# Loading two 128-row weight slabs per transfer, and softmax in one piece with a two-task lag, in a transformer block on eight cores

## The chip, the cores and the metric

The kernel runs on all 8 NeuronCores of one Trainium2 chip. Each core handles one batch element's half of the rows: cores 2b and 2b+1 share batch element b, and each owns 1024 of its 2048 tokens (interleaved blocks of 128). There is no communication between cores; each core computes K and V for all 2048 tokens itself. The metric is device time in microseconds of the slowest core.

A core has a matrix engine (PE; its weight loads are shown as PEld), a vector engine (DVE), a scalar engine (ACT), a general engine (POOL, GpSimd) and a sync engine (SP). In this kernel SP and POOL issue all the DMAs. SBUF is the on-chip memory, PSUM the eight banks into which PE accumulates.

## The reference

For x of shape (4, 2048, 4096), 16 heads of 256:

```python
q, k, v = x @ Wq, x @ Wk, x @ Wv              # rotary on the first 64 of the 256 of each head of q, k
logits  = einsum('bhqd,bhkd->bhqk', q, k)     # causal mask, then / sqrt(256)
out     = einsum('bhqk,bhkd->bhqd', softmax(logits), v)
x = layernorm(x + out @ Wo)
w = kernel * 2.0 - 1.0                        # kernel is a matrix of booleans
x = layernorm(x + scale * (x @ w))
```

The weights are 4096 x 4096, float32 (the last one one byte per entry). Softmax is over up to 2048 keys, with the maximum subtracted.

## The kernel before

Two arenas of SBUF are cut up by hand: `A` holds bfloat16 activations, `B` (`Bu`, `Bf`, `Bb` are views of it as bytes, float32 and bfloat16) holds staging buffers. The order of the work is written out in one walk through the program; each engine gets its instructions in the order of that walk and waits on semaphores for named milestones, so every engine, and each of the two DMA-issuing queues (SP and POOL), runs strictly in that order.

**Projections (lines 239 to 402).** The transposed input, 32 slabs of 128 rows by 2048 tokens, is loaded by POOL in 128 transfers of 128 x 512 float32 into two alternating buffers, and ACT casts each piece to bfloat16 in `A` (L247), where it stays. Then, for each of 8 pairs of heads, five blocks follow: Q, K of either head, V for tokens 0 to 1023, V for tokens 1024 to 2047. A block is 32 steps (`kk`). A step loads a weight slab of 128 rows (SP; 128 x 512 float32 for Q and V, 128 x 256 for K) into one of two staging buffers, DVE casts it into one of two bfloat16 buffers (L269, L320, L371), and PE runs 8 matmuls of 512 columns on it, one for each PSUM bank (L278, L330, L380). The load of step kk waits for the cast of kk-2; the cast waits for its load and for the matmuls of kk-2. After step 31 DVE copies the eight banks to SBUF (L291, L343, L393), and POOL writes the result to DRAM (`qspill`, `kspill`, `vspill`). The first cast of the next block stands behind those eight copies on DVE. During the first Q block the matmuls also wait for the cast of the input slab.

**Attention (lines 407 to 622).** A task is one head and one block of 128 queries, `jj` = 0 to 7; it has (jj+1) x 128 keys in either of two halves P = 0, 1. Logits of both halves go to four PSUM banks (`PL`), the masks being added by a matmul with an identity (L479, L490). DVE takes the negated maximum of each half (L504, L507) and the minimum of the two (L522); ACT computes exp of each half with its row sum (L530); DVE adds the sums (L536), takes the reciprocal (L540) and scales (L546, with bf16 in and out). Three tasks later PE transposes the result in groups of four (L569), DVE copies each group (L579), PE multiplies with V (L592) into two banks, and ACT copies these out (L601). The logits of half P wait for exp of half P of the task before. Q, K and V of a head are loaded two heads ahead by POOL, which also does the rotary arithmetic, six operations of 64 x 1024 and 64 x 2048 per head (L438 to L455), beginning at task jj = 3.

**Output projection, norm, FFN, norm (lines 624 to 908).** Wo (L645, L653) and the FFN weight (L805, L813) are worked through like the projection weights, 8 blocks of 32 steps, with 256 KB (Wo) or 64 KB (FFN) per load, and the cast on ACT. The eight banks of a block are combined with the residual by DVE (L675, L841), whose loads stand in SP's queue ahead of the next block's weights. Between and after them, two passes normalise the rows.

Of the kernel before, what the change touches and what calls it, by code (L numbers as in the profile page):

```python
# [96 lines left out]
def build_nc(taps=()):  # L97
# [100 lines left out]
    def walk():  # L198
# [52 lines left out]

        for p in range(8):
            h0 = 2 * p
            for kk in range(KD):
                b = kk % 2
                if kk >= 2:
                    w = [("qcast", p, kk - 2)]
                elif p > 0:
# [6 lines left out]
                wc = [("qwd", p, kk)]
                if kk >= 2:
                    wc.append(("qmm", p, kk - 2))
                op("vector",
                   lambda e, b=b: e.tensor_copy(Bb[:, WQBF + b * 512:WQBF + (b + 1) * 512],  # L269
                                                Bf[:, WQST + b * 512:WQST + (b + 1) * 512]),  # L270
                   waits=wc, ms=("qcast", p, kk))
# [760 lines left out]
```

How the kernel before makes its waits and increments, by code:

```python
    def op(self, engname, fn, waits=(), inc=None, ms=None):  # L62
        if self.mode == "count":
            for k in waits:
                assert k in self.ms, f"wait on undefined milestone {k}"
            if inc is not None:
                s, n = inc
                self.cnt[s] = self.cnt.get(s, 0) + n
                if ms is not None:
                    for k in (ms if isinstance(ms, list) else [ms]):
                        assert k not in self.ms, f"dup milestone {k}"
                        self.ms[k] = (s, self.cnt[s])
            else:
                assert ms is None, ms
            return
        if engname != self.engname:
            return
        for k in waits:
            s, v = self.ms[k]
            if v > self.waited.get(s, 0):
                self.eng.wait_ge(self.sems[s], v)
                self.waited[s] = v
        instr = fn(self.eng)
        if inc is not None:
            s, n = inc
            instr.then_inc(self.sems[s], n)
# [1 line left out]
    def final_wait(self, engname, semname):  # L88
        if self.mode == "count" or engname != self.engname:
            return
        v = self.cnt.get(semname, 0)
        if v > self.waited.get(semname, 0):
            self.eng.wait_ge(self.sems[semname], v)
            self.waited[semname] = v
```

## Time and profile before

| | us |
|---|---|
| three timed runs | 5691.8, 5708.56, 5713.06 |
| the profiled execution, its own time | 5640.55 |
| its span on the slowest core (core 6) | 5639.0 |
| spans of the other cores | 5549.1 to 5633.0 |
| PE, DVE, ACT, POOL busy on core 6 | 4048.0, 1579.5, 686.4, 611.0 |

All durations below are from the profiled execution, on core 6. A time of the form 3509.66 is a position in it, in us from its start. A busy PE is not a PE at its peak, since its matmuls overlap and their ends are modelled: the granted clock of a stretch (1.00 is 2.4 GHz, 0.50 is 1.2 GHz) and the number of matmuls that fit into it say more. Idle time of an engine counts only where the others wait for it.

### The profile page before, as it was taken

The numbers are of one execution on the slowest core, as the hardware profiler recorded it, in microseconds if no ns is written. First come the engines' busy times: TensorE is split into PE (matmuls) and PEld (weight loads), VectorE is DVE, ScalarE is ACT, GpSimd is POOL, SyncE is SP. The second block draws the span as 40 slices with busy tenths as digits, with TensorE's granted clock in tenths as the row PEclk, the third lists the DMA queues.
The fourth block names the chain that finished last, engine by engine and source line by source line (L and its number), as shares of the span: only waits on it lengthen the run. The fifth ranks groups of instructions, "written<-read, shape, count | busy, mean of one in ns | idle before, by whom it ended". The sixth has DMA issues, their size and how long they took to land.

```text
span 5639.0 us, 60269 instructions; the slowest of 8 cores (5549.1 to 5639.0 us)
## 1 busy us (share of the span) xinstructions
PE 4048.0 (72%) x19074; PEld 1861.7 (33%) x19074; DVE 1579.5 (28%) x3310; ACT 686.4 (12%) x1505; POOL 611.0 (11%) x644
## 2 busy tenths in 40 slices
PE   3369898998988889898994555555587773488850
PEld 0123343333333333333332343333433331233320
DVE  0012222222222222222223555555401114322222
ACT  2210000000000000000001222222222222222210
POOL 2200000000000000000004333333000001100011
PEclk6579999889889999988886676667799996699975
DMA  4433434244342433424233111111055555422246
GB/s 130 128 99 116 133 105 137 84 120 122 99 134 85 136 114 115 135 91 132 88 114 108 44 44 53 56 44 44 1 157 166 167 170 178 131 91 90 90 128 188
DMA packets 349225, 615.17 MB, mean 109 GB/s; under 512 B 41970, under 2 KB 140274, under 8 KB 346866
## 3 DMA queue, kind: packets, MB, share of 16 engines
q1 hardware_dynamic: 295666, 420.45, 26.0%
q0 software_dynamic: 53248, 190.88, 9.7%
q8 instruction: 159, 2.61, 0.2%
q14 instruction: 152, 1.25, 0.1%
HBM read 495.81 MB, written 109.05 MB: 107 GB/s over the span
## 4 chain that ended last, share of the span: by engine, by line
PE 48%; DMA 26%; DVE 11%; issue 8%; ACT 6%; DVEq 0%; POOL 0%; SPq 0%; ACTq 0%; POOLq 0%
PE PL L330 9%; PE pb L330 9%; DMA arenaB<-wo 7%; DMA arenaB<-wv 6%; PE PL L380 5%; PE pb L380 5%; DMA arenaB<-wq 5%; DMA arenaB<-xT 4%; PE PL L813 4%; PE PL L479 4%; PE pb L813 4%; PE pb L592 3%; DMA out<-arenaB 2%; ACT arenaB L530 2%; PE pb L569 1%
## 5 line engine op out<-in xcount | busy, mean ns | idle before, releaser
L380 PE MATMUL PL<-arenaB,arenaA 128*128 128x512 bf16 x2048 | 575.0, 407 | 109.6 <-DVE arenaB L371 108.1
L330 PE MATMUL PL<-arenaA,arenaB 128*128 128x512 bf16 x2048 | 573.5, 406 | 86.7 <-DVE arenaB L320 86.7
L330 PE MATMUL pb<-arenaA,arenaB 128*128 128x512 bf16 x2048 | 568.6, 403 | 0.0
L380 PE MATMUL pb<-arenaB,arenaA 128*128 128x512 bf16 x2048 | 566.2, 402 | 0.0
L530 ACT ACTIVATE arenaB<-PL,arenaB 128x128 bf16<-128x128 f32 (+7 forms) x256 | 188.8, 750 | 2727.7 <-DVE arenaB L522 2727.7
L278 PE MATMUL PL<-arenaA,arenaB 128*128 128x512 bf16 x1024 | 305.7, 427 | 293.1 <-ACT arenaA L247 219.8
L371 DVE CAST arenaB<-arenaB 128x512 bf16<-128x512 f32 x512 | 217.0, 426 | 757.9 <-DMA arenaB<-wv 479.8
L320 DVE CAST arenaB<-arenaB 128x256 bf16<-128x256 f32 x512 | 148.9, 293 | 778.7 <-PE pb L330 722.0
L653 PE MATMUL PL<-arenaB,arenaA 128*128 128x512 bf16 x1024 | 273.2, 390 | 119.4 <-ACT arenaB L645 79.8
L813 PE MATMUL PL<-arenaB,arenaA 128*128 128x512 bf16 x1024 | 272.9, 390 | 93.6 <-DVE arenaB L831 38.4
L380 PEld LDWEIGHTS PL<-arenaB,arenaA 128*128 128x128 bf16 x2048 | 200.7, 102 | 408.7 <-issue 273.7
L330 PEld LDWEIGHTS PL<-arenaA,arenaB 128*128 128x128 bf16 x2048 | 209.2, 103 | 365.3 <-issue 203.9
L479 PE MATMUL PL<-arenaA 128*128 128x512 bf16 (+3 forms) x528 | 175.2, 475 | 192.7 <-ACT arenaB L530 144.3
L278 PE MATMUL pb<-arenaA,arenaB 128*128 128x512 bf16 x1024 | 303.2, 424 | 0.0
L330 PEld LDWEIGHTS pb<-arenaA,arenaB 128*128 128x128 bf16 x2048 | 210.3, 103 | 275.2 <-issue 110.2
L380 PEld LDWEIGHTS pb<-arenaB,arenaA 128*128 128x128 bf16 x2048 | 210.3, 103 | 275.4 <-issue 102.2
L269 DVE CAST arenaB<-arenaB 128x512 bf16<-128x512 f32 x256 | 108.5, 427 | 652.2 <-PE pb L278 376.6
L813 PE MATMUL pb<-arenaB,arenaA 128*128 128x512 bf16 x1024 | 270.2, 386 | 0.7 <-DVE arenaB L841 0.6
L653 PE MATMUL pb<-arenaB,arenaA 128*128 128x512 bf16 x1024 | 269.6, 387 | 0.0
L278 PEld LDWEIGHTS PL<-arenaA,arenaB 128*128 128x128 bf16 x1024 | 99.4, 104 | 466.5 <-issue 390.8
L592 PE MATMUL pb<-arenaA 128*128 128x128 bf16 x1584 | 145.8, 267 | 123.4 <-DVE arenaA L579 91.7
L645 ACT CAST arenaB<-arenaB 128x512 bf16<-128x512 f32 x256 | 158.0, 617 | 435.2 <-DMA arenaB<-wo 395.4
(95 smaller groups left out, 3491.6 us busy)
## 6 DMA issues: line engine op xcount, KB each, us to landing
arenaB<-wv SPq DMA_DIRECT2D x512, 256.0 KB, 2.9
arenaB<-wq SPq DMA_DIRECT2D x256, 256.0 KB, 2.9
arenaB<-wk SPq DMA_DIRECT2D x512, 128.0 KB, 2.1
arenaB<-wo SPq DMA_DIRECT2D x256, 256.0 KB, 2.9
arenaB<-xT POOLq DMA_DIRECT2D x128, 256.0 KB, 3.8
z_hbm<-arenaB POOLq DMA_DIRECT2D x128, 256.0 KB, 3.5
arenaB<-z_hbm SPq DMA_DIRECT2D x128, 256.0 KB, 3.4
kspill<-arenaB POOLq DMA_DIRECT2D x16, 1024.0 KB, 6.8
```

The lines of the kernel that those rows point to most:

```text
L269: lambda e, b=b: e.tensor_copy(Bb[:, WQBF + b * 512:WQBF + (b + 1) * 512], Bf[:, WQST + b * 512:WQST + (b + 1) * 512]),
L278: lambda e, b=b, m=m, n=n, kk=kk: e.matmul(bank(m * 2 + n), Bb[:, WQBF + b * 512 + m * 128:WQBF + b * 512 + (m + 1) * 128], A[:, kk * 2048 ...
L320: lambda e, b=b: e.tensor_copy(Bb[:, WKBF + b * 256:WKBF + (b + 1) * 256], Bf[:, WKST + b * 256:WKST + (b + 1) * 256]),
L330: lambda e, b=b, m=m, n=n, kk=kk: e.matmul(bank(m * 4 + n), Bb[:, WKBF + b * 256 + m * 128:WKBF + b * 256 + (m + 1) * 128], A[:, kk * 2048 ...
L371: lambda e, b=b: e.tensor_copy(Bb[:, WVBF + b * 512:WVBF + (b + 1) * 512], Bf[:, WVST + b * 512:WVST + (b + 1) * 512]),
L380: lambda e, b=b, c=c, bidx=bidx, kk=kk: e.matmul(bank(bidx), A[:, kk * 2048 + c * 128:kk * 2048 + (c + 1) * 128], Bb[:, WVBF + b * 512:WVB ...
L479: qb=qb, kb=kb, jj=jj, stop=stop, AR=AR: e.matmul(PL[:, pbase + coff:pbase + coff + csz], AR[:, qb + m * 1024 + jj * 128:qb + m * 1024 + ( ...
L530: op("scalar", lambda e, P=P, KW=KW, SVX=SVX, AUB=AUB: e.activation(Bb[:, AUB + P * KW:AUB + (P + 1) * KW], PL[:, P * 1024:P * 1024 + KW], ...
L592: lambda e, dh=dh, c=c, kk=kk, KK=KK, vb=vb, AT=AT, AR=AR: e.matmul(avP[dh][:, 0:128], AR[:, vb + c * 256 + dh * 128:vb + c * 256 + (dh + ...
L645: lambda e, b=b: e.copy(Bb[:, WOBF + b * 512:WOBF + (b + 1) * 512], Bf[:, WOST + b * 512:WOST + (b + 1) * 512]),
L653: lambda e, m=m, b=b, kk=kk: e.matmul(bank(m), A[:, CAT0 + kk * 1024 + m * 128:CAT0 + kk * 1024 + (m + 1) * 128], Bb[:, WOBF + b * 512:WOB ...
L813: lambda e, m=m, b=b, kk=kk: e.matmul(bank(m), A[:, X2T0 + kk * 1024 + m * 128:X2T0 + kk * 1024 + (m + 1) * 128], Bb[:, FWBF + b * 512:FWB ...
```

## The change

1. Projections, Wo and FFN: a step loads and casts two slabs (256 rows) at once, with twice the bytes per transfer and twice the columns per cast, and 16 matmuls follow; the number of steps per block falls from 32 to 16. There are still two staging buffers and two cast buffers, each twice as large. The input comes in 64 transfers of 128 x 1024.
2. The staging area for K results is one buffer instead of two, and V results are written to DRAM after each half of a pair (four writes of half the size instead of two).
3. Attention: one maximum over both halves, one exp over both halves with one sum; the minimum of two maxima and the sum of two sums are gone. The logits of both halves wait for the whole exp of the task before.
4. Attention: transposes and V matmuls follow two tasks after the logits instead of three, and ACT's copy-out of a task stands behind the exp of the newer task instead of ahead of it.

On ACT, at the start of attention, before (L530 is exp, L601 the copy-out; both halves and both banks are counted together):

```order
L530 ACTIVATE arenaB<-PL,arenaB 128x128 x2
L530 ACTIVATE arenaB<-PL,arenaB 128x256 x2
L530 ACTIVATE arenaB<-PL,arenaB 128x384 x2
L601 CAST arenaA<-pb 128x128 x2
L530 ACTIVATE arenaB<-PL,arenaB 128x512 x2
L601 CAST arenaA<-pb 128x128 x2
L530 ACTIVATE arenaB<-PL,arenaB 128x640 x2
```

and after (L544 is exp, L613 the copy-out):

```order
L544 ACTIVATE arenaB<-PL,arenaB 128x256
L544 ACTIVATE arenaB<-PL,arenaB 128x512
L544 ACTIVATE arenaB<-PL,arenaB 128x768
L613 CAST arenaA<-pb 128x128 x2
L544 ACTIVATE arenaB<-PL,arenaB 128x1024
L613 CAST arenaA<-pb 128x128 x2
L544 ACTIVATE arenaB<-PL,arenaB 128x1280
```

The rows look alike, but the first copy-out before is that of task 0, emitted in the same turn as the exp of task 3, which follows it; after, it is also that of task 0, but emitted in the turn of task 2, whose exp stands ahead of it. So an exp no longer stands behind the V matmuls that PE runs in the same turn.

On DVE, within one head, before:

```order
L540 RECIPROCAL arenaB<-arenaB 128x1
L546 TENSOR_SCALAR arenaA<-arenaB 128x256
L504 TENSOR_REDUCE arenaB<-PL 128x1
L507 TENSOR_REDUCE arenaB<-PL 128x1
L579 COPY arenaA<-pb 128x512 x3
L579 COPY arenaA<-pb 128x256
L522 TENSOR_TENSOR arenaB<-arenaB 128x1
L536 TENSOR_TENSOR arenaB<-arenaB 128x1
L540 RECIPROCAL arenaB<-arenaB 128x1
L546 TENSOR_SCALAR arenaA<-arenaB 128x512
```

and after:

```order
L550 RECIPROCAL arenaB<-arenaB 128x1
L556 TENSOR_SCALAR arenaA<-arenaB 128x256
L527 TENSOR_REDUCE arenaB<-PL 128x1
L589 COPY arenaA<-pb 128x512 x4
L550 RECIPROCAL arenaB<-arenaB 128x1
L556 TENSOR_SCALAR arenaA<-arenaB 128x512
```

Two reductions have become one over both halves, the two TENSOR_TENSORs are gone, and the group copies are those of the task two back, not three.

The diff, cut to its core (the K and V blocks change as the Q block does, the FFN weights as Wo):

```diff
-        for ii in range(128):
-            kk, qq = ii // 4, ii % 4
+        for ii in range(64):
+            kk, hf = ii // 2, ii % 2
             b = ii % 2
-            w = [("xcast", ii - 2)] if ii >= 2 else [("tabq",)]
-            dma("gpsimd", Bf[:, XST + b * 512:XST + (b + 1) * 512],
-                xT_d[kk * 128:(kk + 1) * 128, qq * 512:(qq + 1) * 512],
+            w = [("xcast", ii - 2)] if ii >= 2 else []
+            dma("gpsimd", Bf[:, XST + b * 1024:XST + (b + 1) * 1024],
+                xT_d[kk * 128:(kk + 1) * 128, hf * 1024:(hf + 1) * 1024],
                 waits=w, ms=("xdma", ii))
...
-            for kk in range(KD):
-                b = kk % 2
-                if kk >= 2:
-                    w = [("qcast", p, kk - 2)]
+            for k2 in range(16):
+                b = k2 % 2
+                if k2 >= 2:
+                    w = [("qcast", p, k2 - 2)]
...
+                dma("sync", Bf[:, WQST + b * 1024:WQST + (b + 1) * 1024].rearrange("p (c m) -> p c m", m=512),
+                    wq_d[k2 * 256:(k2 + 1) * 256, h0 * HD:h0 * HD + 512].rearrange("(c p) m -> p c m", p=128),
+                    waits=w, ms=("qwd", p, k2))
+                wc = [("qwd", p, k2)]
+                if k2 >= 2:
+                    wc.append(("qmm", p, k2 - 2))
                 op("vector",
+                   lambda e, b=b: e.tensor_copy(Bb[:, WQBF + b * 1024:WQBF + (b + 1) * 1024],
+                                                Bf[:, WQST + b * 1024:WQST + (b + 1) * 1024]),
+                   waits=wc, ms=("qcast", p, k2))
+                for sub in range(2):
+                    kk = 2 * k2 + sub
...
+                for hh in range(2):
+                    h = h0 + hh
+                    dma("gpsimd",
+                        vspill[h].rearrange("p (c d) -> p c d", d=HD)[:, ps * 8:(ps + 1) * 8, :],
...
-            wlog.append(("expp", t - 1, P) if t > 0 else p1done)
+            wlog.append(("exp", t - 1) if t > 0 else p1done)
...
             op("vector", lambda e, KW=KW, SVX=SVX: e.reduce_max(
-                   Bf[:, SVX:SVX + 1], PL[:, 0:KW], axis=AX.X, negate=True),
-               waits=wmx, ms=("mxa", t))
-            op("vector", lambda e, KW=KW, SVX=SVX: e.reduce_max(
-                   Bf[:, SVX + 1:SVX + 2], PL[:, 1024:1024 + KW], axis=AX.X, negate=True),
-               waits=[("lgp", t, 1), ("mxa", t)], ms=("mxb", t))
+                   Bf[:, SVX:SVX + 1],
+                   PL.rearrange("p (c k) -> p c k", k=1024)[:, :, 0:KW],
+                   axis=AX.XY, negate=True),
+               waits=wmx, ms=("mx", t))
...
+            op("scalar", lambda e, KW=KW, SVX=SVX, AUB=AUB: e.activation(
+                   Bb[:, AUB:AUB + 2 * KW].rearrange("p (c k) -> p c k", k=KW),
+                   PL.rearrange("p (c k) -> p c k", k=1024)[:, :, 0:KW],
+                   AF.Exp, bias=Bf[:, SVX:SVX + 1], scale=1.0,
+                   accum_out=Bf[:, SVX + 5:SVX + 6]),
+               waits=wexp, ms=("exp", t))
...
-        for u in range(T2 + 3):
+        for u in range(T2 + 2):
...
-            if u - 3 >= 0:
-                emit_trav(u - 3)
+            if u - 2 >= 0:
+                emit_trav(u - 2)
             if u < T2:
                 emit_smx(u)
+            if u - 2 >= 0:
+                emit_avev(u - 2)
...
-            for kk in range(KD):
-                b = kk % 2
-                if kk >= 2:
-                    w = [("wocast", nn, kk - 2)]
+            for k2 in range(16):
+                b = k2 % 2
+                if k2 >= 2:
+                    w = [("wocast", nn, k2 - 2)]
```

## Rows read from the trace of the kernel before

**Rows 1.** The cores of the profiled execution: span, and mean granted TensorE clock.

```profile
core 4: 5558.1 us, clock 0.838
...
core 6: 5639.0 us, clock 0.811
```

**Rows 2.** Stretches of core 6: busy us (x instructions) PE, PEld, DVE, ACT, POOL; granted clock, DMA share, GB/s.

```profile
0.00:349.00 349.00, 114.72 (x259) 33.44 (x260) 19.48 (x47) 79.99 (x129) 69.09 (x132) 0.57 0.44 124
349.00:2993.00 2644.00, 2379.85 (x9984) 1006.80 (x9982) 642.35 (x1550) 0.00 (x0) 38.72 (x46) 0.91 0.38 114
...
3042.00:4073.00 1031.00, 565.90 (x4333) 391.19 (x4332) 558.81 (x1072) 239.64 (x756) 339.00 (x194) 0.66 0.13 45
```

**Rows 3.** Single blocks of 256 matmuls (K, Q, K, Wo), columns as in rows 2.

```profile
1007.00:1065.00 58.00, 57.48 (x255) 25.52 (x256) 9.41 (x33) 0.00 (x0) 1.43 (x2) 0.95 0.28 87
...
934.00:1002.00 68.00, 59.83 (x256) 25.09 (x256) 13.15 (x32) 0.00 (x0) 2.26 (x2) 0.95 0.51 151
1070.00:1138.00 68.00, 67.21 (x256) 27.82 (x256) 9.66 (x33) 0.00 (x0) 0.71 (x1) 0.81 0.26 82
4167.00:4231.00 64.00, 59.30 (x256) 23.73 (x256) 2.19 (x4) 19.14 (x31) 1.22 (x3) 0.98 0.52 154
```

**Rows 4.** First block, timeline: start us, us, engine, line, op, out<-in, [idle before <-releaser].

```profile
106.73 1.21 ACT L247 CAST arenaA<-arenaB 128x512 bf16<-128x512 f32 x2 [3.58 <-DMA arenaB<-xT]
...
107.96 1.13 POOL L210 DMA_DIRECT2D arenaB<-xT  x2 [3.66 <-ACT arenaA L247]
112.31 0.62 ACT L247 CAST arenaA<-arenaB 128x512 bf16<-128x512 f32 x1 [4.37 <-DMA arenaB<-xT]
```

**Rows 5.** Projection blocks after the first, DMA issues: queue, count, KB each, median us to landing.

```profile
arenaB<-wv SPq DMA_DIRECT2D x512, 256.0 KB, 2.9
arenaB<-wk SPq DMA_DIRECT2D x510, 128.0 KB, 2.1
...
qspill<-arenaB POOLq DMA_DIRECT2D x16, 512.0 KB, 4.4
```

**Rows 6.** Between two projection blocks, timeline.

```profile
796.63 2.48 DVE L343 CAST arenaB<-PL 128x512 bf16<-128x512 f32 x4 [3.23 <-PE pb L330]
...
801.42 0.75 DVE L371 CAST arenaB<-arenaB 128x512 bf16<-128x512 f32 x2
...
801.98 0.58 PE L380 MATMUL PL<-arenaB,arenaA 128*128 128x512 bf16 x1 [5.53 <-DVE arenaB L371]
```

**Rows 7.** Matmul groups: line, engine, op, out<-in, xcount | busy, mean ns | idle before <-releaser.

```profile
L380 PE MATMUL PL<-arenaB,arenaA 128*128 128x512 bf16 x2048 | 575.0, 407 | 109.6 <-DVE arenaB L371 108.1
L330 PE MATMUL PL<-arenaA,arenaB 128*128 128x512 bf16 x2048 | 573.5, 406 | 86.7 <-DVE arenaB L320 86.7
...
L278 PE MATMUL PL<-arenaA,arenaB 128*128 128x512 bf16 x1024 | 305.7, 427 | 293.1 <-ACT arenaA L247 219.8 <-DVE arenaB L269 72.9
```

**Rows 8.** One attention task of 256 keys per half, timeline.

```profile
3508.16 0.42 DVE L507 TENSOR_REDUCE arenaB<-PL 128x1 f32<-128x256 f32 x1
...
3509.66 2.41 PE L592 MATMUL pb<-arenaA 128*128 128x128 bf16 x28
...
3512.48 0.49 ACT L530 ACTIVATE arenaB<-PL,arenaB 128x256 bf16<-128x256 f32 x1
...
3513.20 0.48 PE L479 MATMUL PL<-arenaA 128*128 128x384 bf16 x2 [1.14 <-ACT arenaB L530]
```

**Rows 9.** Attention, twelve heads, DVE groups by shape.

```profile
L522 DVE TENSOR_TENSOR arenaB<-arenaB 128x1 f32<-128x1 f32 x96 | 52.4, 546 | 0.0
...
L536 DVE TENSOR_TENSOR arenaB<-arenaB 128x1 f32<-128x1 f32 x97 | 46.5, 480 | 307.9 <-ACT arenaB L530 307.9
...
L504 DVE TENSOR_REDUCE arenaB<-PL 128x1 f32<-128x1024 f32 x12 | 14.7, 1222 | 0.0
```

**Rows 10.** Attention, twelve heads, ACT groups by shape.

```profile
L530 ACT ACTIVATE arenaB<-PL,arenaB 128x1024 bf16<-128x1024 f32 x25 | 27.7, 1117 | 0.0
```

**Rows 11.** Between two Wo blocks, timeline.

```profile
4167.16 1.44 PE L653 MATMUL PL<-arenaB,arenaA 128*128 128x512 bf16 x3 [11.83 <-ACT arenaB L645]
```

More of the change, by code:

```diff
@@ new lines, in walk @@
+                wc = [("wod", nn, k2)]
+                if k2 >= 2:
+                    wc.append(("womm", nn, k2 - 2))
+                op("scalar",
+                   lambda e, b=b: e.copy(Bb[:, WOBF4 + b * 1024:WOBF4 + (b + 1) * 1024],
+                                         Bf[:, WOST4 + b * 1024:WOST4 + (b + 1) * 1024]),
+                   waits=wc, ms=("wocast", nn, k2))
+                for sub in range(2):
+                    kk = 2 * k2 + sub
+                    for m in range(8):
+                        wmm = [("wocast", nn, k2), p2done]
+                        if kk == 0 and nn > 0:
+                            wmm.append(("zev", nn - 1, m))
+                        op("tensor",
+                           lambda e, m=m, b=b, sub=sub, kk=kk: e.matmul(
+                               bank(m),
+                               A[:, CAT0 + kk * 1024 + m * 128:CAT0 + kk * 1024 + (m + 1) * 128],
+                               Bb[:, WOBF4 + b * 1024 + sub * 512:WOBF4 + b * 1024 + (sub + 1) * 512],
+                               start=(kk == 0), stop=(kk == KD - 1)),
+                           waits=wmm if (kk == 0 or m == 0) else (),
+                           ms=("womm", nn, k2) if (m == 7 and sub == 1) else None)
@@ new lines, in walk @@
+                wc = [("fwd", nn, k2)]
+                if k2 >= 2:
+                    wc.append(("fmm", nn, k2 - 2))
+                op("scalar",
+                   lambda e, b=b: e.copy(Bb[:, FWBF6 + b * 1024:FWBF6 + (b + 1) * 1024],
+                                         Bu[:, FWST6 + b * 1024:FWST6 + (b + 1) * 1024]),
+                   waits=wc, ms=("fwcast", nn, k2))
+                for sub in range(2):
+                    kk = 2 * k2 + sub
+                    for m in range(8):
+                        wmm = [("fwcast", nn, k2), x2tall]
+                        if kk == 0 and nn > 0:
+                            wmm.append(("z2ev", nn - 1, m))
+                        op("tensor",
+                           lambda e, m=m, b=b, sub=sub, kk=kk: e.matmul(
+                               bank(m),
+                               A[:, X2T0 + kk * 1024 + m * 128:X2T0 + kk * 1024 + (m + 1) * 128],
+                               Bb[:, FWBF6 + b * 1024 + sub * 512:FWBF6 + b * 1024 + (sub + 1) * 512],
+                               start=(kk == 0), stop=(kk == KD - 1)),
+                           waits=wmm if (kk == 0 or m == 0) else (),
+                           ms=("fmm", nn, k2) if (m == 7 and sub == 1) else None)
```

365 lines of the change are left out of this document (161 added, 204 removed).

## The prediction

> **What bounds the kernel now.** I read the cores first [rows 1]: their spans follow the granted clock, and core 6, at 0.811, sets the end, 81 us behind core 4. Then the stretches of core 6 [rows 2]. The reader is to see three regimes. Up to 349 us PE is busy a third of the time while 128 input pieces come in: that is the first Q block. From 349 to 2993 us PE is busy 90%, at clock 0.91: 39 more blocks of 256 matmuls. From 3042 to 4073 us, 128 attention tasks at 8.05 us each, every engine is idle nearly half the time or more, PE at 0.66 clock: a chain of waits, no full engine.
>
> Single blocks [rows 3] say what is left in the dense stage. A K block takes 57.5 us at 0.95, which is PE's own pace (256 x 0.213 at full clock, plus a slow start). The same block at 0.81 takes 67.2. The Q block shown is 68 us long with only 59.8 of PE busy: 8 us of waiting for weights. The Wo block is 64 us with 4.7 idle. K loads are half as large and land in 2.1 us, Q and V loads in 2.9 [rows 5]. With two buffers, load plus cast (2.9 + 0.43 and a wait or two) come to 3.5 us or so, and the two steps of PE that have to hide them last 3.4. So Q, V and Wo stand exactly at the edge, K does not.
>
> **The change, part by part.**
>
> *Input and first Q block.* The chain of a buffer is cast, issue, transfer, cast. In [rows 4] two casts run from 106.73, the first ends at 107.35, POOL starts the next transfers at 107.96 (0.6 later), and the next cast starts at 112.31. Over the block a pair of pieces costs (349 - 6 for the gap that ends it - 17 for the start, my estimate) / 64 = 5.1 us. After, 32 pairs of 512 KB are left. The nearest row for such a transfer is the Q spill, two of 512 KB one behind the other on the same queue: 4.4 us each [rows 5]. The cast of 1024 columns I take as 0.62 + 512 x 0.82 ns = 1.04 us; the slope is that of exp between 256 columns (0.49) [rows 8] and 1024 (1.117) [rows 10]. A pair is then 0.6 + 4.4 + 1.04 = 6.0; I take 6.5, since weights now share the engines in larger pieces. 32 x 6.5 = 208 against 326: **-115 us**. Bounds: -130 (6.0, nothing shared), -40 (if the rate stays near the 124 GB/s of rows 2).
>
> The Trainium skill's page "DMA: Bandwidth & Descriptors", section "Anatomy of one DMA", gives a transfer from POOL 2.0 us plus its bytes at 436 GB/s. By that 512 KB would land in 3.2 us and this term would be -155; but it gives 2.6 us for 256 KB, where rows 4 show 4.35 from issue to cast, so the rows decide.
>
> *Weight stalls.* A line through 128 KB in 2.1 and 256 KB in 2.9 [rows 5] puts 512 KB at 4.5 us, as the spill row has it. Load, cast (two slabs: at most the 0.75 of the pair in rows 6) and waits make about 5.5 us, and two steps of 16 matmuls last 6.8. The stall goes; what is late next is PE itself. How much it is worth: PE idles 86.7 us ahead of K matmuls, all of it gaps between 16 blocks, 5.4 each [rows 7]. V has as many blocks and 109.6, thus 23 of stalls; Q has 72.9 besides the input's 219.8, less 7 gaps of 5.4, thus 35. Idle below the resolution of the pipelined records and the slower clock after a stall come on top: the Q block of rows 3 is 10 us longer than the K block and shows 8 of it as idle, and V blocks stretch without showing it. I take 75. Bounds 40 (58 less what the spills still cost) and 90. **-75 us.**
>
> *Gaps between blocks.* The eight copies of 0.62 stay, the first cast behind them doubles [rows 6]: at most +0.3 for Q and V, +0.15 for K, over 39 gaps **+8 us** (0 to 12). The halved V write and the single K staging buffer add waits on transfers that were issued a block (about 60 us) earlier; the evictions and casts behind them on DVE, and PE behind those, would stand if they were late, but the spill of rows 5 lands in 4.4 us: 0.
>
> *Attention.* Rows 8 show the chain of one task: V matmuls to 3512.07, copy-out, exp from 3512.48, next logits at 3513.20. PE waits 1.13 us here for work that belongs to the other half of the pipeline. After, exp of a task waits only for its maximum and runs beside transposes and V matmuls; PE goes from the last V matmul straight into the next logits. Removed per head of 8 tasks: the step from V matmul to exp, 8 x 0.41 = 3.3; exp of one half until the logits start, 8 x 0.23 plus the eight exps (0.28 + 0.82 ns a column, 4608 columns: 6.0), 7.9. Then the TENSOR_TENSORs on single columns: they take 0.15 and average 0.546 and 0.480 [rows 9], presumably because GpSimd's rotary operations hold them up; 8 x (0.40 + 0.33) = 5.8, of which I count 5. Sum -16.2. Added: the maximum of both halves now starts after both logits. One at 1024 keys takes 1.222 [rows 9], one at 256 takes 0.42 [rows 8], so 0.15 + 1.045 ns a column: +4.8 per head at most; but the second maximum often stood behind the first, or behind the held-up scaling, so I count +2.2. And in tasks 3 to 6 the double exp (0.28 + 1.64 ns per key) lasts longer than the short V product beside it: +1.5. Sum **-12.5 us per head, x 16 = -200**. Bounds: -100 (all 4.8 exposed, held-up scalings as costly as both TENSOR_TENSORs were, exp over the V product by 3), and -290 (PE also gets the full clock: the logits of a head are 18,432 columns, 7.7 us at 2.4 GHz and 15.4 at 1.2). What is late next is PE through logits, transposes and V product, with the maximum and the group copies on DVE in the middle.
>
> *Wo.* A block gets from 64 to 58.6, 8 x 5.4 = -43. Its gap gets longer: PE waits 11.83 us for the first cast [rows 11], whose load is issued behind the residual's loads; 1.6 more to land and 0.4 to cast, 8 x 2.0 = +16. **-27** (-45 to -10).
>
> *FFN.* Loads of 64 KB were hidden, so nothing to gain; +0.9 in each gap for the larger first cast and load: **+7** (0 to 15). The norm passes are unchanged.
>
> Sum: -115 - 75 + 8 - 200 - 27 + 7 = -402 us. The profiled execution took 5640.5, so it would take 5238. It lies 68 us under the median of the timed runs, 5708.6; I subtract from the median and predict **5305 us**.
>
> **The rivals.**
>
> *The clock takes it back (slower).* At 0.81 a block costs 67.2 instead of 57.5 [rows 3], 9.7 us. There are 56 dense blocks (40 projection, 8 Wo, 8 FFN); core 6 ends 81 us behind core 4 [rows 1], which is what 8 such blocks cost. If denser matmuls bring 0.81 to the other 48, that is +466: 5305 + 466 = 5771, slower. It decides from 41 more blocks (402 / 9.7). For it: the second K block of rows 3 shows that the dense stages are subject to it. Against: full-clock blocks already run at PE's pace, so the change makes them little denser, and the 5.5 us gaps stay.
>
> The Trainium skill's page "TensorE: Matmul & The Clock Gate", section "Part 1: The HAM clock gate", says that a whole die goes to 13/16 of the clock once three of its cores run dense matmuls, and stays there while the load lasts. By that rule all four cores of a die would already stand at 0.81 throughout; rows 3 with two K blocks of one core at 0.95 and 0.81 do not bear that out, and so I leave this rival a small chance.
>
> *Attention gives half or less.* For it: at 640 keys and more per half the double exp and the whole maximum come to over 4 us in series behind the logits. Against: the short chain of rows 8 disappears in every task. It gives 5405.
>
> *Transfers do not scale.* If two 512 KB transfers land no faster per byte than four of 256 KB, the input gives 40 and stalls 30 of their 75: +120, 5425. Against: K's 2.1 and the spill's 4.4.
>
> *Attention at full clock.* Shorter gaps on PE keep it at 2.4 GHz: -60 to -90 more, 5230.
>
> **How the numbers follow.** The forecast as it stands 0.56; attention half or transfers not scaling 0.22 together; full clock 0.16; the clock rival 0.04; something unseen that ends near zero 0.02. Bounds of the terms, taken at their ends together, give 5140 and 5540; nobody expects them all at once, so the range is 5200 to 5440. Three timed runs span 21 us, so 0.5% (28 us) is about what can be told from no change. Faster by more than that 0.94, within 0.02, slower 0.04.
>
> **What would show it.** First Q block: PE's idle time on ACT's input casts from 219.8 to about 110, and the block ending near 235 us. Loads of 512 KB landing in 4 to 5 us. Q and V blocks as long as K's at equal clock, near 57.5. Attention near 830 us, exp no longer behind the copy-out, PE going from V matmul to logits in under 0.3 us in long tasks. Gaps ahead of Wo near 14 us. The prediction is wrong if transfers of 512 KB need 6 us or more, if logits still wait for exp over 1 us in most tasks, or if over half the blocks take 67 us.

## The result, and the profile after

The changed kernel took 5256.56 us in the median of 9 runs (4962.88 to 5603.46), the kernel before 5710.81 (10 runs, 5592.54 to 5924.43). Both medians contain executions in which some cores had a lower clock; the ratio leaves these out: **0.8825, 95% interval 0.8693 to 0.8957**. On the median of before, 5708.56, that is 5038 us: 671 less, where the forecast was 402 less, and outside its range. The direction was right, the size was not.

The cores, as in [rows 1]:

```profile
core 2: 4961.3 us, clock 0.880
...
core 7: 4942.7 us, clock 0.881
```

All eight end within 19 us of each other. In the profile of before, core 6 spent 586 us at a granted clock of 0.8125 and core 4 none, which are the 81 us between them. So the two profiled spans differ by 678 us, but only 597 of it (core 4's 5558.1 to core 2's 4961.3) can come from the edit. I account for these 597.

The stretches of core 2, columns as in [rows 2]: first block, 39 blocks, the way to the first logits, attention, the start of Wo, Wo, norm pass, FFN, end.

```profile
0.00:234.00 234.00, 98.98 (x253) 30.63 (x258) 16.79 (x31) 68.14 (x65) 34.13 (x68) 0.70 0.62 186
234.00:2690.50 2456.50, 2226.66 (x9784) 992.61 (x9984) 542.64 (x928) 0.00 (x0) 51.98 (x62) 0.96 0.40 123
2690.50:2736.00 45.50, 0.90 (x7) 0.43 (x6) 4.88 (x8) 0.00 (x0) 25.11 (x17) 0.56 0.29 89
2736.00:3429.00 693.00, 446.05 (x4428) 333.68 (x4475) 425.31 (x704) 222.07 (x510) 343.57 (x194) 0.85 0.19 66
...
3435.50:4002.00 566.50, 455.35 (x2007) 203.84 (x2048) 75.37 (x112) 132.75 (x127) 30.30 (x56) 0.91 0.56 171
4002.00:4211.00 209.00, 37.59 (x257) 22.33 (x258) 117.29 (x233) 45.00 (x82) 38.87 (x72) 0.51 0.58 177
4211.00:4766.00 555.00, 459.49 (x2007) 204.30 (x2046) 103.73 (x169) 131.47 (x127) 30.22 (x56) 0.91 0.28 85
4766.00:4961.00 195.00, 0.14 (x1) 0.00 (x0) 52.71 (x103) 3.98 (x16) 39.38 (x72) 0.51 0.60 189
```

The same stretch of attention in before, on the undisturbed core 4:

```profile
2947.00:3999.00 1052.00, 559.26 (x4443) 396.35 (x4474) 573.21 (x1088) 243.40 (x766) 338.46 (x194) 0.67 0.13 44
```

The reader is to see the fourth row of after beside this one. PE, DVE and ACT are busy for fewer us, GpSimd for as many as before. PE's 4,400 matmuls shrink from 559 to 446 us, though no matmul went: the granted clock rose from 0.67 to 0.85. The span shrank by 359, more than any engine's busy time did. What went is mostly waiting.

Against the terms of the sum (core 4 of before, core 2 of after; a block is from its first weight load to its last, means):

| term | before | after | measured | forecast |
|---|---|---|---|---|
| first Q block | 315.8 | 208.2 | -108 | -115 |
| 7 Q, 16 V, 16 K blocks | 63.76, 60.22, 56.98 | 56.83, 56.83, 56.88 | -104 | -75 |
| 39 gaps (Q, K, V) | 6.03, 6.04, 6.11 | 6.16, 6.22, 6.42 | +9 | +8 |
| attention, first logits to last V matmul | 1052.5 | 693.4 | **-359** | **-200** |
| Wo stage (block, gap) | 62.97, 12.92 | 56.71, 16.07 | -28 | -27 |
| FFN stage (block, gap) | 57.6, 12.99 | 57.2, 13.86 | +3 | +7 |

Together -587; the other 10 lie in the start, the last gap and the end, a few us each. Over all cores the median of attention goes from 1042 to 692 us, -350; the experiments below use these medians, with 16 heads of 8 tasks in each.

The DMA issues, as in [rows 5], with the input pieces:

```profile
arenaB<-wv SPq DMA_DIRECT2D x256, 512.0 KB, 4.1
arenaB<-wq SPq DMA_DIRECT2D x128, 512.0 KB, 4.3
arenaB<-wk SPq DMA_DIRECT2D x256, 256.0 KB, 2.8
arenaB<-wo SPq DMA_DIRECT2D x128, 512.0 KB, 4.1
arenaB<-xT POOLq DMA_DIRECT2D x64, 512.0 KB, 4.9
```

And PE's matmul groups, as in [rows 7]:

```profile
L402 PE MATMUL PL<-arenaB,arenaA 128*128 128x512 bf16 x2007 | 540.0, 390 | 95.8 <-DVE arenaB L391 93.6
L347 PE MATMUL PL<-arenaA,arenaB 128*128 128x512 bf16 x2006 | 539.7, 390 | 91.1 <-DVE arenaB L335 88.9
...
L291 PE MATMUL PL<-arenaA,arenaB 128*128 128x512 bf16 x1005 | 287.2, 410 | 158.3 <-ACT arenaA L258 109.9
```

The idle time on the input casts is 109.9, from 219.8. V now idles about as long as K (95.8 and 91.1), which is gaps alone. The mean matmul fell from 407 to 390 ns in V, but also in K, which had no stalls (406 to 390): that is core 6's time at 0.8125. The same two groups of before on core 4, which had none of it:

```profile
L380 PE MATMUL PL<-arenaB,arenaA 128*128 128x512 bf16 x2007 | 542.7, 392 | 124.8 <-DVE arenaB L371 121.1 <-issue 0.2
L330 PE MATMUL PL<-arenaA,arenaB 128*128 128x512 bf16 x2006 | 540.0, 391 | 88.9 <-DVE arenaB L320 86.7 <-issue 0.2
```

So V's gain is mainly idle time, not clock. Only the Q blocks had a lower clock too: on core 4 the granted clock in them was 0.944 in the mean against 0.962 in the K blocks, and all blocks of core 2 have 0.963 or 0.964 after.

Then the pipeline itself, the timeline of core 2 from a long task (1024 keys a half; the V product at 3035.66, beside its exp, is that of the task two before) into tasks of 128 and 256 keys a half:

```profile
3028.23 4.05 POOL L475 TENSOR_TENSOR arenaB<-arenaB,tabks 64x2048 bf16<-64x2048 bf16 x1
3028.72 4.04 DVE L556 TENSOR_SCALAR arenaA<-arenaB 128x1792 bf16<-128x1792 bf16 x1
...
3032.68 2.28 DVE L527 TENSOR_REDUCE arenaB<-PL 128x1 f32<-128x2048 f32 x1
...
3035.05 1.97 ACT L544 ACTIVATE arenaB<-PL,arenaB 128x2048 bf16<-128x2048 f32 x1 [5.48 <-DVE arenaB L527]
...
3035.66 1.50 PE L602 MATMUL pb<-arenaA 128*128 128x128 bf16 x24
...
3037.25 0.43 ACT L613 CAST arenaA<-pb 128x128 bf16<-128x128 f32 x2
3037.26 0.27 PE L502 MATMUL PL<-arenaA 128*128 128x128 bf16 x2
...
3038.66 0.47 ACT L544 ACTIVATE arenaB<-PL,arenaB 128x256 bf16<-128x256 f32 x1 [0.98 <-DVE arenaB L527]
...
3039.54 1.72 PE L602 MATMUL pb<-arenaA 128*128 128x128 bf16 x28
...
3041.10 0.38 PE L502 MATMUL PL<-arenaA 128*128 128x256 bf16 x2
...
3041.35 0.43 ACT L613 CAST arenaA<-pb 128x128 bf16<-128x128 f32 x2 [2.12 <-PE pb L602]
```

Exp (L544) waits for the maximum and for nothing else, and is over when the V product (L602) ends; the next logits (L502) start as soon as the V product is through, beside the copy-out (L613), where [rows 8] show 1.1 us between them. 28 V matmuls took 2.41 us there and take 1.72 here, at a higher clock. The first two rows show where DVE is still held up longest: a scaling of some 0.7 us that takes 4.04 and ends 0.5 us after GpSimd's rotary operation.

### The profile page after: what moved, and what is told of

Same layout as the page of the kernel before. It is cut to its first block, busy times and chain, and to the rows that moved or that the text cites. A ratio compares the mean times of both kernels' runs of the same rounds, so it can differ in the third digit from the quotient of the medians.

```text
span 4961.3 us, 52305 instructions; the slowest of 8 cores (4942.7 to 4961.3 us)
## 1 busy us (share of the span) xinstructions
PE 3725.5 (75%) x18740; PEld 1788.0 (36%) x19074; DVE 1338.7 (27%) x2286; ACT 604.9 (12%) x929; POOL 593.6 (12%) x596
## 4 chain that ended last, share of the span: by engine, by line
PE 71%; DMA 9%; DVE 9%; issue 6%; ACT 3%; POOL 0%; another core or an unknown queue 0%; DVEq 0%; SPq 0%; ACTq 0%; POOLq 0%
PE PL L402 9%; PE PL L347 9%; PE pb L402 9%; PE pb L347 9%; PE PL L833 5%; PE PL L670 5%; PE pb L833 5%; PE pb L670 5%; PE PL L291 4%; PE pb L291 4%; PE PL L502 4%; DMA arenaB<-xT 3%; PE pb L602 3%; DMA out<-arenaB 2%; DVE arenaB L527 2%
## 5 line engine op out<-in xcount | busy, mean ns | idle before, releaser
L402 PE MATMUL PL<-arenaB,arenaA 128*128 128x512 bf16 x2007 | 540.0, 390 | 95.8 <-DVE arenaB L391 93.6
L347 PE MATMUL PL<-arenaA,arenaB 128*128 128x512 bf16 x2006 | 539.7, 390 | 91.1 <-DVE arenaB L335 88.9
L347 PE MATMUL pb<-arenaA,arenaB 128*128 128x512 bf16 x2007 | 533.2, 386 | 2.7 <-issue 0.7
L402 PE MATMUL pb<-arenaB,arenaA 128*128 128x512 bf16 x2008 | 532.9, 386 | 2.4 <-issue 0.2
L544 ACT ACTIVATE arenaB<-PL,arenaB 128x256 bf16<-128x256 f32 (+7 forms) x128 | 156.3, 1221 | 2879.2 <-DVE arenaB L527 2873.0
L291 PE MATMUL PL<-arenaA,arenaB 128*128 128x512 bf16 x1005 | 287.2, 410 | 158.3 <-ACT arenaA L258 109.9
L670 PE MATMUL PL<-arenaB,arenaA 128*128 128x512 bf16 x1003 | 268.6, 389 | 116.3 <-ACT arenaB L660 100.8
L391 DVE CAST arenaB<-arenaB 128x1024 bf16<-128x1024 f32 x256 | 176.1, 693 | 657.9 <-PE pb L402 597.6
L833 PE MATMUL PL<-arenaB,arenaA 128*128 128x512 bf16 x1003 | 271.6, 392 | 99.7 <-ACT arenaB L823 72.7
L335 DVE CAST arenaB<-arenaB 128x512 bf16<-128x512 f32 x256 | 107.7, 426 | 718.3 <-PE pb L347 686.0
L291 PE MATMUL pb<-arenaA,arenaB 128*128 128x512 bf16 x1003 | 286.6, 410 | 1.3 <-issue 0.4
L833 PE MATMUL pb<-arenaB,arenaA 128*128 128x512 bf16 x1004 | 267.8, 387 | 1.1
L670 PE MATMUL pb<-arenaB,arenaA 128*128 128x512 bf16 x1004 | 266.5, 386 | 1.1
L527 DVE TENSOR_REDUCE arenaB<-PL 128x1 f32<-128x256 f32 (+7 forms) x128 | 173.6, 1356 | 173.0 <-PE pb L579 131.7
L280 DVE CAST arenaB<-arenaB 128x1024 bf16<-128x1024 f32 x128 | 88.2, 694 | 468.4 <-PE pb L291 411.3
L210 POOL DMA_DIRECT2D z_hbm<-arenaB x128 | 69.1, 540 | 1192.2 <-DVE arenaB L851 530.8
L579 PE MATMUL pb<-identb,arenaA 128*128 128x128 bf16 x1152 | 108.9, 233 | 109.3 <-DVE arenaA L589 109.3
```

The source lines that it names most:

```text
L291: lambda e, b=b, sub=sub, m=m, n=n, kk=kk: e.matmul(bank(m * 2 + n), Bb[:, WQBF + b * 1024 + sub * 512 + m * 128: WQBF + b * 1024 + sub * ...
L335: lambda e, b=b: e.tensor_copy(Bb[:, WKBF + b * 512:WKBF + (b + 1) * 512], Bf[:, WKST + b * 512:WKST + (b + 1) * 512]),
L347: lambda e, b=b, sub=sub, m=m, n=n, kk=kk: e.matmul(bank(m * 4 + n), Bb[:, WKBF + b * 512 + sub * 256 + m * 128: WKBF + b * 512 + sub * 25 ...
L391: lambda e, b=b: e.tensor_copy(Bb[:, WVBF + b * 1024:WVBF + (b + 1) * 1024], Bf[:, WVST + b * 1024:WVST + (b + 1) * 1024]),
L402: lambda e, b=b, sub=sub, c=c, bidx=bidx, kk=kk: e.matmul(bank(bidx), A[:, kk * 2048 + c * 128:kk * 2048 + (c + 1) * 128], Bb[:, WVBF + b ...
L527: op("vector", lambda e, KW=KW, SVX=SVX: e.reduce_max(Bf[:, SVX:SVX + 1], PL.rearrange("p (c k) -> p c k", k=1024)[:, :, 0:KW], axis=AX.XY ...
```

## The experiments

Each is told by its attention stage, median over the cores, because the stages are independent (shown by att_all, below). Clock means the granted clock in that stretch, also the median over the cores; a single row shows that of its core. The edits of the attention are three: the **order** (exp ahead of the copy-out on ACT), the **merge** (one maximum and one exp over both halves in place of two, with the TENSOR_TENSORs gone), and the **lag** (two tasks in place of three between logits and V product).

**order_only.** Before, with the copy-out behind exp.

```diff
+        def emit_avev(t):            # the two copy-outs, out of emit_trav
...
                 emit_smx(u)
+            if u - 3 >= 0:
+                emit_avev(u - 3)
```

> The kernel before, with one edit in attention: ACT's copy-out of a task stands behind the exp of the newest task; lag of three tasks, split maximum and split exp stay. The attention stage lasts 1053 us before (core 4) and 693 after the whole change. Theory A (the step from V matmul to exp on ACT was the chain, the rest is small): 780 us or less. Theory B (the parts need each other: exp still waits for the minimum of the maxima, which stands behind the group copies on DVE): only the step V matmul to exp (0.65 us x 8) and the part of exp that fits beside the V matmuls (about 4 us per head) go, 9 us per head, so 905 us.

Measured: 838 us, -204. Core 4:

```profile
2959.40:3792.10 832.70, 486.73 (x4446) 348.60 (x4479) 536.38 (x1088) 243.31 (x766) 341.77 (x195) 0.77 0.16 55
```

It lies between the two theories (780 or less, 905). The order is the largest part, but not all; DVE is as full as before (536 against 573), and the clock is halfway (median 0.76).

**merge_only.** Before, with one maximum and one exp.

```diff
-            op("vector", ... e.reduce_max(..., PL[:, 0:KW], axis=AX.X, negate=True), ...
-            op("vector", ... e.reduce_max(..., PL[:, 1024:1024 + KW], axis=AX.X, negate=True), ...
+            op("vector", ... e.reduce_max(..., PL.rearrange("p (c k) -> p c k", k=1024)[:, :, 0:KW], axis=AX.XY, ...
-            op("vector", ... e.tensor_tensor(..., ALU.min), ...
-            for P in range(2):
+            op("scalar", ... e.activation(..., AF.Exp, bias=Bf[:, SVX:SVX + 1], ...
-            op("vector", ... e.tensor_add(...), ...
```

> The kernel before, with one edit in attention: one maximum and one exp over both halves; copy-out ahead of exp and lag of three stay. Theory A: the two TENSOR_TENSORs that GpSimd holds up are gone, 6 us per head, so about 960 us. Theory B: exp still stands behind the copy-out, and is now twice as long ahead of the next logits (+6 us per head and 0.2 x 8), the maximum is later by up to 4.8, against 6 of held-up TENSOR_TENSORs: 1053 to 1130 us, no gain or slower.

Measured: 960 us, -82, clock 0.73: the figure of theory A. The longer maximum and the longer exp cost less than the removed instructions and their hold-ups gave. In the prediction these parts (-5, +2.2 and +1.5 per head) come to -1.3 per head, or -21 us.

**lag_only.** Before, with a lag of two.

```diff
-            if u - 3 >= 0:
-                emit_trav(u - 3)
+            if u - 2 >= 0:
+                emit_trav(u - 2)
```

> The kernel before, with one edit in attention: transposes and V matmuls follow two tasks after the logits instead of three. Both theories: the same work stands in the same chain, 1053 us within 25. If the lag by itself were the cause, it would be under 1000.

Measured: 1041 us, within 1 us of before, clock 0.65.

**att_all.** Before, with the whole attention change, and nothing else of the edit.

> The kernel before with the whole attention change and its own projections, Wo and FFN. If the stages are independent: attention 693 us within 15, the rest as before, so about 360 us less than before on an undisturbed core. If the larger transfers or the clock of the stages around it had a part in the attention gain: over 720 us.

Measured: 692 us, as in the changed kernel, clock 0.85; what follows attention took 1581 us against 1564 to 1571 in the three runs above. So the input, weight and Wo parts of the edit have no share in the 350, and its size has to be explained within the attention. The whole time fell by less than the 360 expected: the four cores without 0.8125 took 5233 to 5268 us, some 300 less than core 4 of before, mostly because first logits came at 2978 to 2985 us there and not at 2947. The old projections vary like this: over the cores without 0.8125 of all runs that have them, the first block took 288 to 333 us, a Q block 63.5 to 66.3 and a V block 59.8 to 61.5. In the changed kernel these are 202 to 217, and 56.7 to 56.9 for both.

**after_copy_first** and **after_lag3.** The changed kernel, each with one part undone.

```diff
-            if u < T2:
-                emit_smx(u)
             if u - 2 >= 0:
                 emit_avev(u - 2)
+            if u < T2:
+                emit_smx(u)
```

> The changed kernel, with one edit undone: the copy-out of a task stands ahead of the exp of the newest task on ACT. Attention lasts 691 us in the changed kernel; the copy-out order alone took 205 of 1043 from the kernel before, the merging alone 82. Theory interaction (with the merged exp the order is worth more, as the whole 352 is 65 more than the parts): 950 to 970 us, as with merging alone. Theory sum (the parts add): 690 + 205 = 895.

```diff
-            if u - 2 >= 0:
-                emit_trav(u - 2)
+            if u - 3 >= 0:
+                emit_trav(u - 3)
             if u < T2:
                 emit_smx(u)
-            if u - 2 >= 0:
-                emit_avev(u - 2)
+            if u - 3 >= 0:
+                emit_avev(u - 3)
```

> The changed kernel with the lag of three tasks of before. By lag_only (no difference) 691 us of attention within 15. Rival: now that exp runs beside the V product, the pairing counts; with lag two the longest V products stand beside the two shortest exps, with lag three beside the first three and the longest exp beside a short one: +1.5 us per head, 715 us.

Measured: 996 us (+304, more than either expectation) and 720 us (+28, outside the 15 that lag_only had led me to expect, and near the 715 of the rival). The timeline of after_copy_first, core 2:

```profile
3205.28 1.01 PE L602 MATMUL pb<-arenaA 128*128 128x128 bf16 x8 [1.38 <-DVE arenaA L589]
3206.38 0.43 ACT L613 CAST arenaA<-pb 128x128 bf16<-128x128 f32 x2 [5.13 <-PE pb L602]
3206.70 1.13 ACT L544 ACTIVATE arenaB<-PL,arenaB 128x1024 bf16<-128x1024 f32 x1
...
3208.06 1.23 PE L502 MATMUL PL<-arenaA 128*128 128x512 bf16 x4 [1.77 <-ACT arenaB L544]
3208.29 2.02 DVE L556 TENSOR_SCALAR arenaA<-arenaB 128x1024 bf16<-128x1024 bf16 x1
```

V product, copy-out, exp and logits are again one chain, and now the whole exp of both halves (1.13 us, at 1024 keys in all) stands in it, where the split one let PE start after the first half.

With these the effect can be taken apart in one order: before 1042, with the order 838, with the merge as well 720 (after_lag3), with the lag as well 692. That is -204, -118, -28. The merge is worth 82 with the old order and 118 with the new. The lag is worth 1 alone, 28 in the changed kernel, and costs 36 with the merge but the old order (960 to 996). **The parts do not add up one by one**: 204 + 82 + 1 = 287.

**before_no_rotary** and **after_no_rotary.** Is it GpSimd that holds DVE up, and how much of the gain is that?

```diff
-            op("gpsimd", ... e.tensor_mul(Bb[0:64, 7168:9216], AR[0:64, kb:kb + 2048], tabkc[:, :]), ...
+            op("gpsimd", ... e.tensor_mul(Bb[0:64, 7168:7170], AR[0:64, kb:kb + 2], tabkc[:, 0:2]), ...
```

(likewise the other five rotary operations of each head, so all but two columns of Q and K enter the logits unrotated)

> The kernel before with GpSimd's six rotary operations per head cut to two columns each (their DMAs stay), so Q and K are not rotated. Theory GpSimd (DVE's scalings and TENSOR_TENSORs are held up beside them, in tasks 5 and 6 of a head, 10.8 and 12.9 us long where 6.9 and 7.8 would be in line): 9 us per head less, attention about 900 us instead of 1043, and tasks 5 and 6 at 7 to 8 us. Rival (these tasks are long for their size): over 1000.

> The changed kernel with the same six operations cut to two columns. If the change got rid of most of the hold-ups (no TENSOR_TENSORs, the scaling beside logits): 691 down to 660 to 675, so that about 110 of the 352 us gained are hold-ups that went. If the hold-ups are as costly as before: down by 140, to 550.

Measured: 886 us (-156 against 1042) and 668 us (-24 against 692), both as the GpSimd theory had them. The hold-up can be seen in the timeline of before, core 6, DVE and then GpSimd:

```profile
3540.85 1.94 DVE L536 TENSOR_TENSOR arenaB<-arenaB 128x1 f32<-128x1 f32 x1 [2.07 <-ACT arenaB L530]
3542.89 0.16 DVE L540 RECIPROCAL arenaB<-arenaB 128x1 f32<-128x1 f32 x1
3543.16 4.21 DVE L546 TENSOR_SCALAR arenaA<-arenaB 128x1536 bf16<-128x1536 bf16 x1
3547.30 1.08 DVE L504 TENSOR_REDUCE arenaB<-PL 128x1 f32<-128x896 f32 x1
```

```profile
3538.72 4.05 POOL L449 TENSOR_TENSOR arenaB<-arenaA,tabkc 64x2048 bf16<-64x2048 bf16 x1
...
3542.91 4.04 POOL L452 TENSOR_TENSOR arenaB<-arenaB,tabks 64x2048 bf16<-64x2048 bf16 x1
```

An addition of one column takes 1.94 us and ends with the first GpSimd operation shown (both at 3542.8). A scaling starts beside the second and takes 4.21 us, to 0.4 us after that one's end, and the maximum that exp, and so PE's next logits, need is queued behind it. DVE's groups of before (core 4), by shape:

```profile
L522 DVE TENSOR_TENSOR arenaB<-arenaB 128x1 f32<-128x1 f32 x127 | 69.1, 544 | 0.3
...
L546 DVE TENSOR_SCALAR arenaA<-arenaB 128x1536 bf16<-128x1536 bf16 x16 | 56.3, 3516 | 2.1 <-DVE arenaB L540 0.5
L546 DVE TENSOR_SCALAR arenaA<-arenaB 128x1280 bf16<-128x1280 bf16 x16 | 33.7, 2108 | 1.7
```

and of before_no_rotary (core 6):

```profile
L522 DVE TENSOR_TENSOR arenaB<-arenaB 128x1 f32<-128x1 f32 x119 | 17.7, 149 | 0.0
...
L546 DVE TENSOR_SCALAR arenaA<-arenaB 128x1536 bf16<-128x1536 bf16 x15 | 9.3, 620 | 2.0 <-DVE arenaB L540 0.5
L546 DVE TENSOR_SCALAR arenaA<-arenaB 128x1280 bf16<-128x1280 bf16 x15 | 8.3, 553 | 1.6
```

So it is GpSimd; the prediction's "presumably" is shown. And 156 - 24 = 132 us of the 350 are hold-ups that the edit took off the path, with the clock that came back with them (0.67 to 0.75 in before_no_rotary); which of its three parts took them off isn't shown. Some still exist (in after the scaling of 1792 columns takes 3.36 us in the mean, that of 1536 columns 1.41), but they cost only the 24.

**before_filler.** How much of it is the clock? 12 more matmuls of 128 columns per task, which nothing waits for.

```diff
                 emit_trav(u - 3)
+                for i in range(12):
+                    op("tensor", lambda e: e.matmul(pb[0][:, 256:384], identb[:, :], maska[:, :], start=True, stop=True))
```

> The kernel before with twelve matmuls of 128 columns added after the V matmuls of each attention task, into an unused part of a bank; PE runs them while it would wait for the copy-out and exp (a wait of about 1.4 us; they take 0.7 us at full clock, 1.3 at half). In the kernel before attention stands at clock 0.67, in the changed one at 0.85. Theory clock (a third of the gain is that PE, less idle, is granted 2.4 GHz): the clock goes to 0.8 or more and attention gets 40 to 80 us shorter than 1042, with more work. Theory chain only: the clock may rise, but attention stays within 15 us of 1042, since the time is in waits on ACT and DVE.

Measured on core 4:

```profile
2932.50:3945.40 1012.90, 582.72 (x5955) 460.16 (x6004) 559.24 (x1088) 243.12 (x766) 339.55 (x195) 0.80 0.13 46
```

1,536 more matmuls (the trace holds 1,512 of them), and the stage is 28 us shorter (1009 to 1018 on cores 4 to 7, which had no 0.8125; cores 0 to 3 had 1368 to 1794 us of it and are left out). With more to do, PE got 0.80 in place of 0.67. So a busier PE is granted more clock, and that is worth 28 us or more of before's attention; how much more can't be read from this run, since the added matmuls themselves lie partly on the path. The 28 us lie between the two expectations (40 to 80, within 15).

**best1.** The changed kernel with the first load and cast of the next block issued ahead of the evictions of this one, in all dense stages.

```diff
+            if bi + 1 < len(blocks):
+                wload(blocks[bi + 1], 0)
+                wcast(blocks[bi + 1], 0)
+                wload(blocks[bi + 1], 1)
             evict(bk)
...
+            if nn < 7:                 # Wo; FFN likewise
+                wo_lc(nn + 1, 0)
+                wo_lc(nn + 1, 1)
             for m in range(8):
```

> The changed kernel, with the first cast of a projection block ahead of the eight evictions on DVE, and in Wo and FFN the first two loads (and casts) of the next block ahead of the residual's loads. The gaps between blocks are 6.3 us (projections), 16.1 (Wo) and 13.9 (FFN). Theory queue order (the gaps are the cast's and the load's place in their queues): gaps of about 1 us, then PE paced by evictions, 0.6 us a bank in projections and 1.4 to 2 in the others; a period 4 us less in projections, 8 in Wo, 2 in FFN: 39 x 4 + 7 x 8 + 7 x 2 = 226 us less, 4735. Rival (denser matmuls, more of them at 0.81 of the clock, 9.7 us a block): the gain is used up, 4900 to 5000.

Measured: 4840.09 us in the profiled execution against 4962.88, -123. That is half of the 226 expected. First logits come at 2610 in place of 2733 us. Projection gaps went from 6.3 to 1.6 us and blocks grew by 1.4 (by 1.6 in best1_again): 3.1 to 3.3 us a block, 121 to 127 for 39, which is the whole gain. At such a boundary (core 4 of best1_again) PE follows the evictions bank by bank, 0.22 us behind each:

```profile
1007.14 1.03 PE L325 MATMUL pb<-arenaB,arenaA 128*128 128x512 bf16 x4
1009.25 0.38 PE L325 MATMUL PL<-arenaB,arenaA 128*128 128x512 bf16 x1 [1.08 <-DVE arenaB L356]
1009.84 0.38 PE L325 MATMUL PL<-arenaB,arenaA 128*128 128x512 bf16 x1 [0.22 <-DVE arenaB L356]
```

Wo gained little: on core 2 its gap fell from 16.1 to 1.9 us, but each block after the first grew from 56.7 to 69, and the stage went from 566 to 554 us. FFN gained nothing: gap 13.9 to 1.7, block 57.2 to 68.4, stage 555 to 559. The timeline of core 4 of best1 between two Wo blocks:

```profile
3366.16 0.69 DVE L672 TENSOR_TENSOR arenaB<-PL,arenaB 128x512 f32<-128x512 f32 x1 [65.12 <-PE pb L647]
...
3366.96 0.69 DVE L677 BATCH_NORM_STATS2 stats<-arenaB 128x6 f32<-128x512 f32 x1
3367.00 0.38 PE L647 MATMUL PL<-arenaB,arenaA 128*128 128x512 bf16 x1 [1.01 <-DVE arenaB L672]
...
3372.25 0.69 DVE L672 TENSOR_TENSOR arenaB<-pb,arenaB 128x512 f32<-128x512 f32 x1 [0.44 <-DMA z_hbm<-arenaB]
...
3375.48 0.59 PE L647 MATMUL pb<-arenaB,arenaA 128*128 128x512 bf16 x1 [1.81 <-DVE arenaB L672]
```

Each bank comes free only after its residual addition, and DVE has 1.4 us for a bank (0.69 twice), later also a wait for the write of an earlier result. The gap had been waiting for a cast; with that gone, the evictions were next, and they were nearly as late.

**after_again** and **best1_again**, the two kernels beside each other on one chip.

> The changed kernel once more, on the same chip as best1_again, so that the two can be compared with each other. Forecast: its profiled stages repeat within 1%: first logits at about 2735 us, attention 685 to 700 us, a projection block 56.8 us with a gap of 6.2 to 6.4 us behind it.

> The version with the next block's loads and casts issued earlier, beside the changed kernel on one chip. If its gain is the shorter period of the 39 projection blocks (2.9 us each, 113 us in all) and nothing in the other stages, first logits come 120 to 130 us earlier than in the changed kernel here too, and its time is 2.3 to 2.7% shorter. The rival: the first profile of it was taken on another chip, and the 123 us are that chip's; then the two are within 1%.

Measured: ratio to before 0.8874 (0.8831 to 0.8917) for the changed kernel and 0.8672 (0.8627 to 0.8717) for best1; 0.8672 / 0.8874 = 0.977, thus -2.3%. First logits at 2737 and 2616 us. The gain of best1 is real and not another chip's; it beats both kernels.

## Why the prediction was wrong

**The step that failed is the attention term, "Sum -12.5 us per head, x 16 = -200".** Its mechanism was right: exp freed from the copy-out, PE from the V product straight into logits. Its size was not: -22 us per head. It lies beyond the far bound of -290 too. By the parts of a task (core 4 of before, core 2 of after; PE's points are starts of weight loads; means over the heads, summed over the 8 tasks of a head):

| stretch of a task | before | after | difference | forecast |
|---|---|---|---|---|
| first to last weight load of the logits | 13.2 | 10.5 | -2.7 | none |
| from there to the end of the maximum | 21.5 | 16.0 | -5.5 | +2.2, and a part of -5 |
| from there to the last weight load of the V product | 15.9 | 14.3 | -1.6 | +1.5 |
| from there to the next logits | 15.2 | 2.3 | -12.9 | -11.2, and a part of -5 |

1. *The chain behind the V product* was sized about right: 3.3 + 7.9 and part of the 5. order_only and after_copy_first show that it is the chain.
2. *Hold-ups of DVE.* I counted only what [rows 9] show on single columns, 5 us per head. The scalings are held up as well, up to 3.6 us over their length, and the maximum is queued behind them. I had named them ("the held-up scaling") only as cover for the longer maximum. The two no_rotary runs make it 132 / 16 = 8.3 per head, 52 us more than the 80 counted, clock included.
3. *The longer maximum.* Counted +2.2; the stretch became 5.5 shorter. merge_only shows that with the old order too one maximum and one exp win, by 82, where the prediction's terms for them give 21.
4. *The clock.* I kept it for a rival ("attention at full clock", -60 to -90) with 0.16. It rose from 0.67 to 0.85, and the logits, and the stretch up to the last V matmul, which have the same matmuls as before, lost 2.7 + 1.6 per head, 69 us, though not all of that need be the clock. The prediction treated as a separate chance what follows from its own claim: if PE waits less, it is granted more. before_filler shows that link with the waits left in place.
5. *The lag* I gave no value. It is worth 28 us in this combination.

These overlap, and I can't split the 159 us between them exactly: a shorter wait gives clock, and clock shortens the wait. What is shown is the total by parts (204, 118, 28) and the share of the hold-ups (132).

*Weight stalls*: -104 for -75. The steps were right (4.1 to 4.3 us for 512 KB, forecast 4.5; all blocks at K's length). The counted idle time of 58 left out more than I added for it: Q blocks were 6.9 us longer than they are now, and V blocks 3.4. The bound of 90 was too tight as well; core 4 of before is even near the low end of what the other runs show for these blocks (att_all, above).

*Input*: -108 for -115 (32 x 6.5 = 208 against 326 is -118, not -115); idle on the input casts 109.9 for "about 110", the block over at 234 for "near 235". The transfer took 4.9 us and not 4.4, which the 0.5 us of allowance held.

*Gaps, Wo and FFN*: +9, -28 and +3 for +8, -27 and +7. In Wo two errors cancel: the gap is 16.1, not "near 14", and the block 56.7, not 58.6.

*The rivals.* The clock did not take anything back: no core was at 0.81 in the profiled execution, and blocks took 56.8 us, not 67. Transfers scaled. Attention gave more and not less, and its clock rose: the nearest rival was the one on the far side, at 5230, and that was still short of it, as it moved the clock alone. The rival "half or less" rested on 4 us of exp and maximum in series from 640 keys a half; by the prediction's own slopes they are 1.3 + 1.5 us at 640 and 4.2 only at 1024. The near bound of the attention term is off too: with all three of its items it comes to -54, and to -100 only without the last.

*The base.* I subtracted from a median of 5708.56, 150 us above core 4's 5558. With the forecast's own -402 against core 4's 5558 the ratio would have been 0.928; core 2 against core 4 gives 0.893, and the measured ratios are 0.8825 and, in after_again, 0.8874. So the base is not the cause of the miss.

## What to carry to other kernels

Where every engine is half idle, the time of a pipeline is its chain: write down which instruction is queued behind which on the in-order engines, and move what belongs to another task behind what the next step needs. Don't price such a change as a sum of removed instructions: price what is queued behind a held-up one, add the clock that a busier PE is granted, and let the range reach further on the side of gain, since parts worth 204, 82 and 1 alone came to 350 together. Where a gap is about to be closed, look for the second wait that ends as late; in Wo the blocks after the first took back 12 of the 14 us that each gap gave.

## What the runs showed of the hardware

- **A DVE operation can last as long as GpSimd's.** While GpSimd runs a TENSOR_TENSOR (2.1 or 4.05 us), DVE's TENSOR_TENSOR of one column and its TENSOR_SCALAR within SBUF stand until GpSimd's is over; reductions from PSUM (1.08 us beside it), copies from PSUM and reciprocals keep their length. It cost 156 of 1042 us in before and 24 of 692 in after, because the price hung on what was queued behind the held-up instruction. The Trainium skill's page "SBUF — State Buffer", section "Who interferes with whom", says that a DVE instruction with two SBUF inputs, or in a two-port mode, shares ports with a GpSimd instruction that reads SBUF, and that the second to issue waits for the first to end; by that rule, the trace agrees, down to the reductions that are spared.
- **The granted clock answers to the waits.** In attention, with the same matmuls: 0.67 in 1042 us and in 996, 0.73 in 960, 0.76 in 838, 0.81 in 720, 0.85 in 692; and 0.80 in 1014 us with 12 matmuls added per task for which nothing waits.
- **0.8125 comes by pairs of cores and differs between profiles.** Before had 586 us on cores 6 and 7 each and none on cores 4 and 5; att_all had 298 us on cores 4 and 5, 197 on cores 6 and 7 and none on the others; before_filler had 1368 to 1794 us on cores 0 to 3. The changed kernel, whose matmuls stand closer, had none of it on any core in its profile. Whether denser work makes it more or less frequent isn't shown.
- **Loads grow less than their bytes.** With eight cores loading, 128, 256 and 512 KB land in 2.1, 2.8 to 2.9 and 4.1 to 4.3 us on SP's queue.
